# Four graph layers on one core: count one-hots a step further ahead, output projection loads issued earlier, and two convolutions that read their rows from SBUF with the first one's weights split in the stage before

## The chip, the cores and the metric

One core of a Trainium2 chip. The metric is the device time of one execution in microseconds; lower is better. All stretches are given from the start of the profiled span.

## The reference

1250 nodes (padded to 10 tiles of 128), width 768, 20000 edges sorted by target, 34 edge types. Four layers, each followed by a residual and a layer norm:

```python
x = _layernorm(x + _L0(x))   # relu(x W_ah + b), three GAT convolutions of 4 heads, relu(concat @ W_out + b_out)
x = _layernorm(x + _L1(x))   # GCN: h = x @ W; out[col] += dinv[row] * dinv[col] * h[row]; + b
x = _layernorm(x + _L2(x))   # GAT of 12 heads of 64 with a residual projection
x = _layernorm(x + _L3(x))
# _L3:
mean = agg.reshape(N_REL, n, -1) / jnp.maximum(cnt, 1.0).reshape(N_REL, n, 1)
h1 = jnp.einsum('rni,rio->no', mean, W_rel) + x @ W_root + b_rgcn
xw = h1 @ W_gcn
out = jax.ops.segment_sum(xw[src] * norm[:, None], dst, num_segments=n)
out = out + xw * (dinv * dinv)[:, None] + b_gcn
```

## The kernel before

Five engine programs are written out by hand and synchronised by counting semaphores. Between most stages stands `meet` (L165): each engine drains, adds one, and waits for all five. The order of the work is each engine's own program order. The stages, with their rough places in the span:

- **Phase 1** (to 614): `x W_ah`, then the three GAT projections W_H[0..2]. Beside the third, and after it, an N x N table of edge counts is made from 49 groups of 4 x 128 edges. For a group, VectorE makes the source one-hots and type one-hots (`dve_compare`, L796 and L800), ScalarE the target one-hots (`act_targets`, L808, L810), TensorE sums them (`pe_group`, L840, 12 matmuls), ScalarE copies the sum (`act_sums`, L819) and VectorE adds it into the table `ct` (`dve_add`, L827). Per projected tile VectorE also makes the attention reductions (`projected`, L496, L497). Beside each of the last eight tiles there are two groups, one before and one behind the tile's products (L351); 33 groups follow in a loop. VectorE compares one group ahead: group k + 1, then the add of group k.
- **Phase 3 and att0** (to 1242): the table is turned, then 12 heads of attention; POOL stores each head's output into `gat_d` (L1100).
- **Output projection** (`sp_wout`, `act_wout`, `dve_wout`, `pool_wout`; 1242 to 1554): three blocks, l = 0 to 2, each rows `gat_d[l]` times a 768 x 768 block of W_out, added up in `z4` in SBUF. The products are made in split precision: rows and weights are each split in a high and a low part (CAST and subtract, L1433, L1434 by chunks of 128 rows; rows by ScalarE L386 and VectorE L403), and a tile's products are 3 x 6 x 2 = 36 matmuls (L270), behind 6 transposes (L253). SyncE streams row tiles (L221), the next block's weights (L215), and, in the third block, a tile of x (L1414), which waits until an earlier tile is normalised. VectorE empties PSUM (L1458), and in the third block also adds x, norms, and makes a mask (`dve_mask2`, L883) that only the 12-head attention uses. `dve_wout` splits the weights of block 0 first, all six chunks.
- **conv1** (`Convolution`, to 1758): rows x1 are read back from DRAM and transposed; one DMA loads the weights (L209) and VectorE splits them whole (L394, L395); g = dinv * product (L1524, L1567); then the aggregation with count columns (L1554).
- **Heads, att2, root, rel** (to 3716): the 12-head layer and the relation products, which aren't touched, save that the masks come to stand at the front of the heads.
- **Sum** (to 3992): messages are summed into `hbuf` (L1968, L1993). Then `sp_h1` stores h1 to DRAM (L2011), between two meetings.
- **conv3**: the same class as conv1, with rows read back from `h1_d`.

The quoted lines are those that set the order in counting and in the third block:

```python
for k in range(2 * (j - FIRST_TILE), 2 * (j - FIRST_TILE) + 2):
    dve_compare(v, k + 1, (k + 1) % 2)
    dve_add(v, step, k, k % 2)
    if k % 2 == 0:
        projected(2, j, j % 2)
```

## Time and profile before

| what | value |
|---|---|
| median of 3 runs | 4196.65 us (4187.52 to 4201.66) |
| the profiled execution: device time | 4204.77 us |
| its span, first to last instruction | 4203.2 us |
| its mean granted TensorE clock | 0.958 |
| busy in the span | TensorE 3832.1, VectorE 1959.1, ScalarE 1702.1, POOL 1569.5 us |

The profiled execution took 8.1 us more than the median. Busy time is a sum over the span; TensorE's matmuls are pipelined, so that a busy TensorE isn't one at its peak. In a row of a timeline stand the start, the duration, the engine, the line and operation, what is written and read, how many instructions are merged, and in brackets the idle time before it and what ended that.

### The profile page before, as it was taken

To read this page: it belongs to the slowest core of one execution; us is meant where nothing else is said; L and a number is where in the kernel's file an instruction comes from. 1 tells how busy PE (TensorE), PEld (TensorE's weight loads), DVE (VectorE), ACT (ScalarE), POOL (GpSimd) and SP (SyncE) were. 2 spreads that over 40 slices of the span, in tenths; PEclk is the share of its full clock that TensorE was granted. 3 is DMA by queue.
4 is the path that set the end of the run, shared out by engine and by line. 5 is a ranking of instruction groups with operands and counts; after the bars stand their busy time and mean duration, and the time that the engine had idled before them with its cause. 6 is when DMAs were issued, how large, how long until landed. Compare 5 with 4: busy or idle time off the path is not lost. (4 is left out here: it accounts for less than half of the span.)

```text
span 4203.2 us, 58400 instructions
## 1 busy us (share of the span) xinstructions
PE 3832.1 (91%) x18472; PEld 2962.6 (70%) x18473; DVE 1959.1 (47%) x2764; ACT 1702.1 (40%) x2902; POOL 1569.5 (37%) x1191
## 2 busy tenths in 40 slices
PE   8998768999988869869998999999999999989989
PEld 4554336777768859732222699999999999965579
DVE  7245687666633343489996233333333332013325
ACT  1113576766653212149988133333333333310021
POOL 3887873444430000101111244444444444357600
PEclk9998998999998979979999999999999999999989
DMA  4332111222213231231111355555555554368821
GB/s 139 103 106 65 36 23 54 66 66 65 70 53 121 68 108 48 91 106 56 50 50 25 120 184 186 185 184 185 184 180 182 183 181 135 112 221 303 258 86 67
DMA packets 209319, 494.64 MB, mean 118 GB/s; under 512 B 71824, under 2 KB 88231, under 8 KB 209206
## 3 DMA queue, kind: packets, MB, share of 16 engines
q1 hardware_dynamic: 121078, 217.41, 16.0%
q0 software_dynamic: 53568, 181.40, 13.9%
q10 hardware_dynamic: 34560, 94.45, 6.4%
q8 instruction: 56, 0.92, 0.1%
q14 instruction: 57, 0.47, 0.0%
HBM read 365.32 MB, written 127.48 MB: 117 GB/s over the span
## 5 line engine op out<-in xcount | busy, mean ns | idle before, releaser
L1875 PE MATMUL ps<-wsplit,xsplit 128*128 x6840 | 1237.0, 337 | 1.3 <-POOL xsplit L1842 1.3
L1875 PEld LDWEIGHTS ps<-wsplit,xsplit 128*128 128x128 f32 x6840 | 1181.5, 188 | 1.5 <-issue 1.5
L1304 ACT ACTIVATE work<-ps,work 128x418 f32<-128x418 f32 x720 | 435.1, 606 | 241.2 <-PE ps L1214 240.4
L1251 PE MATMUL ps<-hbuf,work 128*128 128x193 f32 x2400 | 494.5, 345 | 13.2 <-DVE work L1166 13.1
L1842 POOL TENSOR_TENSOR xsplit<-ct,xsplit 128x768 fp32r<-128x768 f32 x190 | 370.1, 1948 | 297.6 <-ACTq L1907 297.5
L1149 DVE SCALAR_TENSOR_TENSOR work<-work,cnt 128x1250 f32<-128x1250 f32 x240 | 370.7, 1545 | 229.4 <-ACT work L1304 226.1
L1812 DVE CAST wsplit<-wplain 128x768 fp32r<-128x768 f32 x204 | 115.6, 567 | 761.3 <-PE ps L1875 730.4
L1912 ACT ACTIVATE ct<-ps,invs 128x768 f32<-128x768 f32 x190 | 171.4, 902 | 711.7 <-PE ps L1875 711.7
L1251 PEld LDWEIGHTS ps<-hbuf,work 128*128 128x128 f32 x2400 | 385.3, 191 | 83.3 <-issue 83.3
L1295 ACT ACTIVATE ps<-work,lr 128x418 f32<-128x418 f32 x720 | 418.3, 606 | 5.8 <-DMA work<-lrow_d 5.8
L1837 POOL DMA_INDIRECT ct<-x_d,relrec x190 | 199.1, 1048 | 517.7 <-PE ps L1863 497.3
L1241 PE MATMUL ps<-work,hbuf 128*65 128x512 f32 x720 | 340.4, 556 | 16.7 <-DVE work L1149 16.5
L270 PE MATMUL ps<-wsplit,xsplit 128*128 128x384 f32 x1800 | 343.9, 351 | 12.1 <-DVE xsplit L403 12.1
L270 PEld LDWEIGHTS ps<-wsplit,xsplit 128*128 128x128 f32 x1800 | 330.9, 199 | 14.1 <-DVE xsplit L403 14.1
L1214 PEld LDWEIGHTS ps<-work 3*128 3x128 bf16 x720 | 65.3, 91 | 357.5 <-ACT ps L1295 186.0
L1214 PE MATMUL ps<-work 3*128 3x418 bf16 x720 | 251.8, 351 | 29.3 <-DMA work<-shift_d 26.2
L1348 POOL DMA_INDIRECT invs<-inv_d,relrec x190 | 249.7, 1314 | 65.5 <-issue 57.6
L1968 PE MATMUL ps<-work 128*128 128x384 f32 x784 | 256.1, 490 | 18.8 <-DMA work<-msg_d,work 17.6
L1813 DVE TENSOR_TENSOR wsplit<-wplain,wsplit 128x768 fp32r<-128x768 f32 x204 | 245.9, 1205 | 7.1
L763 POOL DMA_INDIRECT relrec_d<-work x160 | 228.1, 1426 | 48.8 <-issue 48.8
L763 POOL DMA_INDIRECT dstrec_d<-work x160 | 207.0, 1293 | 97.9 <-DVEq L685 49.4
L1968 PEld LDWEIGHTS ps<-work 128*128 128x128 f32 x784 | 149.7, 191 | 124.9 <-issue 23.0
(215 smaller groups left out, 4375.5 us busy)
## 6 DMA issues: line engine op xcount, KB each, us to landing
wplain<-in_L_gnn_W_rel SPq DMA_DIRECT2D x34, 2304.0 KB, 9.7
msg_d<-ct ACTq DMA_DIRECT2D x190, 384.0 KB, 2.6
work<-lrow_d SPq DMA_DIRECT2D x47, 625.0 KB, 3.6
feat_d<-work ACTq DMA_DIRECT2D x30, 386.0 KB, 3.1
hbuf<-feat_d SPq DMA_DIRECT2D x60, 193.0 KB, 2.5
gat_d<-work POOLq DMA_DIRECT2D x12, 960.0 KB, 5.2
xplain<-gat_d SPq DMA_DIRECT2D x30, 384.0 KB, 3.1
work<-xa_d SPq DMA_DIRECT2D x27, 384.0 KB, 3.4
```

Source lines behind the costliest of these rows:

```text
L270: last = pe.matmul(o, x[:, u, c * P:(c + 1) * P], w[:, c * D + h * HALF:c * D + (h + 1) * HALF], start=(q == 0 and c == 0), stop=(q == 2 a ...
L763: g.indirect_dma_start(out=(relrec_d, dstrec_d)[which], out_offset=bass.IndirectOffsetOnAxis(addr[:, which, t:t + 1], 0), in_=(relpay[:, t ...
L1149: v.scalar_tensor_tensor(p[:, 0:N], p[:, 0:N], 1.0, cnt3[:, q % NT, 0:N], ALU.min, ALU.mult).then_inc(self.s_p, 1)
L1214: pe.matmul(ps[:, b, 0:c1 - c0], self.ones3, self.crow[h % 2][:, c0:c1], start=False, stop=True, skip_group_check=True).then_inc(self.s_ad ...
L1241: last = pe.matmul(ps[0:C + 1, 3 + k, 0:n1 - n0], self.feat(h, s), p[:, n0:n1], start=(s == 0), stop=(s == NT - 1))
L1251: last = pe.matmul(ps[:, self.b0 + b, t * (C + 1):(t + 1) * (C + 1)], p[:, dt * P:(dt + 1) * P], self.feat(h, s), start=(s == 0 and t == 0 ...
L1295: act.activation(ps[:, b, 0:c1 - c0], self.Rb[h % 2][:, c0:c1], ACT.Relu, bias=lr[:, col:col + 1]).then_inc(self.s_relu, 1)
L1304: act.activation(self.p[q % 3][:, c0:c1], ps[:, b, 0:c1 - c0], ACT.Exp, bias=self.l2[:, col:col + 1], scale=1.0 - SLOPE)\
L1348: g.indirect_dma_start(out=invs[:, k:k + 1], out_offset=None, in_=inv_d, in_offset=bass.IndirectOffsetOnAxis(relrec[:, 2 * k + 1:2 * k + 2 ...
L1842: g.tensor_tensor(xlo7[:, k % XW, :], xt7[:, k % 2].rearrange("p c n -> p (c n)"), xhi7[:, k % XW, :].bitcast(F32), ALU.subtract).then_inc ...
L1875: last = pe.matmul(ps[:, 4 + 2 * (u % 2) + h, 0:HALF], x[:, u, c * P:(c + 1) * P], w[:, bass.ds(base + (c * D + h * HALF), HALF)], start=( ...
L1968: last = pe.matmul(ps[:, 2 * (u % 2) + h, 0:HALF], sel8[:, GT * (u % 2) + w, :], mg8[:, GT * u + w, h * HALF:(h + 1) * HALF], start=(w == ...
```

## The change

- `dve_compare` is one group further ahead (k + 2 before the add of k).
- Meetings between attention and output projection, between that and conv1, and around the store of h1 are taken out; single waits stand in their place. TensorE opens block 0 before the attention (`open`), and its first transposes come right behind the last attention product.
- SyncE issues the bias columns and row tiles 0 and 1 of block 0 during the last head; the broadcasts of the output bias wait for the last product and the last head's store.
- In block 0 VectorE splits chunk 0, makes the low rows of tile 0, then splits the other five.
- The x tiles of the third block are issued by POOL, behind the x1 store of the tile two before. Into the room of the second projection's weights SyncE loads conv1's weights in pieces (four at tile 0, two at tile 6); VectorE splits one chunk a tile in tiles 3 to 8.
- The ten masks go to the front of the heads stage.
- Both convolutions take their rows from SBUF (`multiply_resident`): conv1 from `z4`, conv3 from `hbuf`. The store and reload of h1 are gone. conv3 splits by chunk.
- Split products run by chunk: six matmuls (two halves, three part products) for a chunk, with a wait for that chunk's split.

```diff
@@ dve_phase1
-            dve_compare(v, 0, 0)
+            for k in range(2):
+                dve_compare(v, k, k)
             for j in range(FIRST_TILE, NT):
                 for k in range(2 * (j - FIRST_TILE), 2 * (j - FIRST_TILE) + 2):
-                    dve_compare(v, k + 1, (k + 1) % 2)
+                    dve_compare(v, k + 2, k % 2)
                     dve_add(v, step, k, k % 2)
@@ class Dense
+            def products(self, pe, j, u):
...
+                    whi, wlo, xhi, xlo, (s_w, s_x), n = self.split
+                    pe.wait_ge(s_x, NT * n + j + 1)
+                    for c in range(KC):
+                        pe.wait_ge(s_w, KC * n + c + 1)
+                        for h in range(2):
+                            for q, (x, w) in enumerate(((xhi, whi), (xhi, wlo), (xlo, whi))):
+                                last = pe.matmul(ps[:, 4 + 2 * u + h, 0:HALF], x[:, u, c * P:(c + 1) * P],
...
@@ sp_wout
+            sp.wait_ge(att0.s_max, NT * att0.H)
+            for u in range(2):
+                sp.wait_ge(att0.s_stored[u], 16 * 2)
             for l in range(3):
                 for j in range(NT):
                     W_OUT[l].stream_tile(sp, j, j % 2, P)
                     if l == 0 and j == 1:
+                        sp.wait_ge(att0.s_agg, NT * att0.H)
+                        for u in range(2):
+                            sp.wait_ge(att0.s_stored[u], 16 * (att0.H // 2))
...
-                    if l == 2:
-                        if j < 2:
-                            sp.wait_ge(W_OUT[1].product, W_OUT[1].all_products)
+                    if l == 2 and j in (0, 6):
+
+                        if j == 0:
+                            sp.wait_ge(s_split4, 3 * KC)
                         else:
-                            sp.wait_ge(s_z4, j - 1)
-                        n = tile_rows(j)
-                        sp.dma_start(x4s[0:n, j % 2, :], a["x"][j * P:j * P + n, :]).then_inc(s_x4s[j % 2], 16)
-            conv1.dense.load(sp)
+                            sp.wait_ge(conv1.s_w, 2)
+                        for c in range(4) if j == 0 else (4, 5):
+                            sp.dma_start(wplain[:, (c % 4) * D:(c % 4 + 1) * D], a["L1_gnn_W"][c * P:(c + 1) * P, :]).then_inc(conv1.dense.w_in, 16)
@@ dve_wout
                     if j + 2 < NT:
                         d.low_rows(v, (j + 2) // 2, j % 2)
+                    elif l == 2 and j == NT - 1:
+                        v.sem_inc(conv1.dense.emptied, 2)
+                        conv1.dense.low_rows(v, 0, 0)
+                    if l == 2 and 3 <= j < 3 + KC:
+                        c = j - 3
...
+                        conv1.dense.split_chunk(v, step, c, wplain[:, (c % 4) * D:(c % 4 + 1) * D])
@@ pool_wout
                 g.dma_start(x1_d[j * P:(j + 1) * P, :], z4[:, j, :]).then_inc(s_z4st[j % 2], 16)
+                if j + 2 < NT:
+                    n = tile_rows(j + 2)
+                    g.dma_start(x4s[0:n, j % 2, :], a["x"][(j + 2) * P:(j + 2) * P + n, :]).then_inc(s_x4s[j % 2], 16)
@@ Convolution.pe, act, dve
-                self.dense.multiply(pe)
+                self.dense.multiply_resident(pe, self.rows, lambda j: self.ready(pe, j))
...
+                    if self.n == 0:
+                        act.wait_ge(s_z4st[u], 16 * (i + 1))
...
-                d.split_weights(v, step)
...
+                if self.n == 1:
+                    v.sem_inc(d.emptied, 2)
+                    v.wait_ge(d.w_in, d.b[d.pick] + 16)
+                    d.split_chunk(v, step, 0, d.w_at[:, 0, :])
+                    d.low_rows(v, 0, 0)
+                    for c in range(1, KC):
+                        d.split_chunk(v, step, c, d.w_at[:, c, :])
+                d.low_rows(v, 0, 1)
```

How the instructions stand now. VectorE, in counting, around the reductions of the first tile with groups beside it; L796, L800 are a group's one-hots, L496, L497 the reductions, L827 the add. Before:

```order
L496 TENSOR_TENSOR work<-work 128x768 [waits dve_step]
L497 TENSOR_REDUCE lr<-work 128x4 [waits dve_step]
L796 TENSOR_TENSOR hbuf<-iota,drec 128x4x34 [waits dve_step,count_products]
L800 TENSOR_SCALAR hbuf<-iota,drec 128x1280 x4
L824 TENSOR_LOAD group_dst
L824 ISA x2
L827 ISA [waits counts_summed]
L827 TENSOR_TENSOR ct<-hbuf,ct 128x1314
```

Now (L799, L803 and the like are the same lines, three or four further down), with the group of the next tile in front of the reductions:

```order
L800 TENSOR_TENSOR hbuf<-iota,drec 128x4x34 [waits count_products]
L804 TENSOR_SCALAR hbuf<-iota,drec 128x1280 x4
L828 TENSOR_LOAD group_dst [waits tables_cleared]
L828 ISA x2
L831 ISA [waits counts_summed]
L831 TENSOR_TENSOR ct<-hbuf,ct 128x1314
L499 TENSOR_TENSOR work<-work 128x768 [waits dve_step,h_tile_ready]
L500 TENSOR_REDUCE lr<-work 128x4 [waits dve_step]
```

The comparison that followed the reductions, and for which TensorE waited, now stands before the add and the reductions.

SyncE in the third block of the output projection (L221 and now L220 are row tiles). Before, one x load after each row tile:

```order
L1414 DMA work<-in_x 128x768 [waits dense_product]
L221 DMA xplain<-gat_d 128x768 [waits dense_turned]
L1414 DMA work<-in_x 128x768 [waits x1_ready]
L221 DMA xplain<-gat_d 128x768 [waits dense_turned]
L1414 DMA work<-in_x 128x768 [waits x1_ready]
```

Now:

```order
L1426 DMA wplain<-in_L_gnn_W 128x768 [waits wout_weights_split]
L1426 DMA wplain<-in_L_gnn_W 128x768 x3
L220 DMA xplain<-gat_d 128x768 [waits dense_turned] x6
L1426 DMA wplain<-in_L_gnn_W 128x768 [waits conv_w_split]
L1426 DMA wplain<-in_L_gnn_W 128x768
L220 DMA xplain<-gat_d 128x768 [waits dense_turned] x3
```

The waits for a normalised tile (x1_ready) have left this queue; two waits for splits have come.

VectorE from the last add of the sum to the second convolution. Before:

```order
L1993 TENSOR_TENSOR hbuf<-ps,hbuf 128x768
L394 CAST wsplit<-work 128x4608 [waits dve_step,met,dense_w_in1]
L395 TENSOR_TENSOR wsplit<-work,wsplit 128x4608 [waits dve_step]
L403 TENSOR_TENSOR xsplit<-xplain,xsplit 128x768 [waits dve_step,dense_product,dense_taken]
L403 TENSOR_TENSOR xsplit<-xplain,xsplit 128x768 [waits dense_product,dense_taken]
```

Now, of the five further chunks the first:

```order
L2031 TENSOR_TENSOR hbuf<-ps,hbuf 128x768
L397 CAST wsplit<-work 128x768 [waits dve_step,dense_w_in1]
L398 TENSOR_TENSOR wsplit<-work,wsplit 128x768 [waits dve_step]
L406 TENSOR_TENSOR xsplit<-xplain,xsplit 128x768 [waits dve_step,dense_product,dense_taken]
L397 CAST wsplit<-work 128x768
L398 TENSOR_TENSOR wsplit<-work,wsplit 128x768 [waits dve_step]
```

The wait for the meeting (met) is gone, and the low rows come after one chunk's split.

## Rows read from the trace of the kernel before

**Rows 1.** Timeline of TensorE in the counting, 430 to 500 us.

```profile
447.51 2.41 PE L840 MATMUL ps<-hbuf 128*128 128x512 bf16 x12
...
453.72 3.90 PE L840 MATMUL ps<-hbuf 128*128 128x512 bf16 x12 [3.15 <-DVE hbuf L800]
457.46 7.90 PE L351 MATMUL ps<-work 128*128 128x384 f32 x24
```

**Rows 2.** Waits of TensorE, 340 to 496: us in total, times, longest.

```profile
PE ps L840 <- DVE hbuf L800: 32.0, 9, 5.5
```

**Rows 3.** Timelines of ScalarE and VectorE at the same place.

```profile
449.96 1.26 ACT L819 ACTIVATE hbuf<-ps 128x1314 uint16<-128x1314 f32 x1 [1.37 <-PE ps L840]
...
452.81 0.30 DVE L796 TENSOR_TENSOR hbuf<-iota,drec 128x136 bf16<-128x136 uint16 x1
```

**Rows 4.** Groups by line, 494 to 614: busy us, mean ns, idle before.

```profile
L840 PE MATMUL ps<-hbuf 128*128 128x512 bf16 (+1 forms) x387 | 79.5, 351 | 40.0 <-DVE hbuf L800 40.0
L800 DVE TENSOR_SCALAR hbuf<-iota,drec 128x1280 bf16<-128x1280 uint16 x128 | 72.9, 630 | 0.0
```

**Rows 5.** Timeline of TensorE, 1225 to 1345.

```profile
1234.40 7.46 PE L1251 MATMUL ps<-hbuf,work 128*128 128x193 f32 x44
...
1280.38 1.54 PE L253 MATMUL ps<-ident,xplain 128*128 128x128 f32 x6 [6.72 <-DMA xplain<-gat_d]
```

**Rows 6.** POOL and SyncE there; the drain (ns); landing (page, DMA issues).

```profile
1245.12 1.01 POOL L1100 DMA_DIRECT2D gat_d<-work  x1 [23.96 <-DVEq L1169]
...
1257.14 9.01 SPq L1403 DMA_DIRECT2D hbuf<-in_L_gnn_b_out  x10
...
L167 POOLq DRAIN  x1: 4075/4075/4075, 1250.4 to 1250.4; - x1
...
gat_d<-work POOLq DMA_DIRECT2D x12, 960.0 KB, 5.2
```

**Rows 7.** The third block as one window: busy times, clock, DMA share, GB/s.

```profile
1423.20:1554.10 130.90, 87.86 (x421) 84.51 (x420) 51.37 (x93) 28.11 (x80) 4.36 (x8) 0.79 0.29 90
```

**Rows 8.** Waits of SyncE's queue, 1423 to 1554.

```profile
SPq L1414 <- DVEq L1466: 114.2, 8, 20.0
```

**Rows 9.** Timeline of TensorE: steady tiles of block two, first of block three.

```profile
1368.89 6.51 PE L270 MATMUL ps<-wsplit,xsplit 128*128 128x384 f32 x36
...
1375.81 6.52 PE L270 MATMUL ps<-wsplit,xsplit 128*128 128x384 f32 x36
...
1431.52 8.77 PE L270 MATMUL ps<-wsplit,xsplit 128*128 128x384 f32 x36 [0.67 <-DVE xsplit L403]
```

**Rows 10.** Timeline of VectorE: a third-block tile, and two chunks' splits.

```profile
1254.49 0.56 DVE L1433 CAST wsplit<-wplain 128x768 fp32r<-128x768 f32 x1 [9.73 <-POOLq L167]
...
1256.08 0.56 DVE L1433 CAST wsplit<-wplain 128x768 fp32r<-128x768 f32 x1
...
1443.60 0.96 DVE L403 TENSOR_TENSOR xsplit<-xplain,xsplit 128x768 fp32r<-128x768 f32 x1 [2.32 <-ACT xsplit L386]
...
1448.73 0.95 DVE L1458 TENSOR_TENSOR hbuf<-ps,hbuf 128x768 f32<-128x768 f32 x1
```

**Rows 11.** DMA issues, 1440 to 1563: KB each, median us to landing.

```profile
x_d<-hbuf POOLq DMA_DIRECT2D x10, 384.0 KB, 5.4
```

**Rows 12.** Timeline of TensorE: the first convolution's first products.

```profile
1572.12 8.09 PE L270 MATMUL ps<-wsplit,xsplit 128*128 128x384 f32 x36 [2.80 <-DVE xsplit L403]
```

**Rows 13.** The chain that ended last: start, us, what.

```profile
3992.78 10.84 DMA h_d<-hbuf
...
4012.66 8.08 PE ps L270 x36
```

**Rows 14.** The masks (ns); POOL and VectorE at the heads.

```profile
L883 DVE TENSOR_SCALAR ct<-ct x10: 489/494/497, 1434.4 to 1553.6; 128x1280 bf16<-128x1280 uint16 x10
...
1762.26 6.60 POOL L1633 MEMSET hbuf<- 128x7800 f32 x1 [0.15 <-POOL work L1631]
...
1777.02 0.96 DVE L496 TENSOR_TENSOR work<-hbuf,work 128x768 f32<-128x768 f32 x1 [13.19 <-ACTq L1703]
```

More of the change, by code:

```diff
@@ L313, in turn @@
                     last.then_inc(self.turned, 1)
-                def times(j):
-                    pe.wait_ge(self.taken, self.b["taken"] + j + 1)
-                    pe.wait_ge(self.emptied, self.b["emptied"] + j + 1)
-                    for h in range(2):
-                        for c in range(KC):
-                            last = pe.matmul(ps[:, 4 + 2 * (j % 2) + h, 0:HALF], self.xt_at[:, j % 2, c, :],
-                                             self.weight(c)[:, h * HALF:(h + 1) * HALF], start=(c == 0), stop=(c == KC - 1))
-                    last.then_inc(self.product, 1)
                 turn(0)
@@ L327, in multiply_resident @@
                         turn(j + 1)
-                    times(j)
+                    self.products(pe, j, j % 2)
             def multiply_single(self, pe, between):
@@ L404, in low_rows, with take_and_empty @@
                  .then_inc(s_x, 1)
-            def take_and_empty(self, act, loop, per, empty, before=None):
-                for u in range(2):
+            def take_and_empty(self, act, loop, per, empty, before=None, taken=0):
+                for u in range(taken, 2):
                     self.take(act, 0, u)
@@ L1444, in dve_wout @@
                 v.sem_inc(d.emptied, 2)
-                for j in range(2):
-                    d.low_rows(v, j // 2, j % 2)
+                if l == 0:
+                    split(0, 0)
+                    d.low_rows(v, 0, 0)
+                    for c in range(1, KC):
+                        split(0, c)
+                    d.low_rows(v, 0, 1)
+                    v.wait_ge(s_root, 1)
+                    step(v.reciprocal(dinv[:, :], dinv[:, :]))
+                else:
+                    for j in range(2):
+                        d.low_rows(v, 0, j)
                 for j in range(NT):
                     z = z4[:, j, :]
-                    if l == 2:
-                        dve_mask2(v, step, j)
                     if l == 1 and j == 6:
                         v.wait_ge(W_OUT[0].product, W_OUT[0].all_products)
+                    if l == 0 and j == 6:
+                        for u in range(2):
+                            v.wait_ge(att0.s_stored[u], 16 * (att0.H // 2))
                     for c in {6: (0, 1), 7: (2, 3), 8: (4,), 9: (5,)}.get(j, ()) if l < 2 else ():
@@ L1468, in pool_wout @@
         def pool_wout(g, step):
+            g.wait_ge(s_split4, 3 * KC)
+            for j in range(2):
+                g.dma_start(x4s[:, j, :], a["x"][j * P:(j + 1) * P, :]).then_inc(s_x4s[j], 16)
             for j in range(NT):
@@ L1510, in sp @@
             def sp(self, sp):
[L1511 removed]
+                sp.wait_ge(self.s_emptied, self.at2 + 1)
                 sp.dma_start(self.brow, self.bias.partition_broadcast(P)).then_inc(self.s_b_in, 16)
@@ L2033, in _ @@
                 W_OUT[0].load_piece(sp, c)
-            meet(sp)
             sp_wout(sp)
-            meet(sp)
+            for u in range(2):
+                sp.wait_ge(s_z4st[u], 16 * (NT // 2))
             conv1.sp(sp)
@@ L2112, in _ @@
             self_loops(v, step, ALU.subtract)
+            for j in range(NT):
+                dve_mask2(v, step, j)
             dve_heads(v, step)
```

168 lines of the change are left out of this document (71 added, 97 removed).

## The prediction

> **What bounds the kernel now.** I read the chain of waits first, then the idle time of TensorE by releaser, then the timelines of the places that the diff touches. TensorE is the engine that the other four feed; what the change can win is idle or slow TensorE time, and there are five places.
>
> *Counting.* Each tile of the third GAT projection has two count groups beside it. The group behind the tile's products runs at once (2.41 us). The next one starts 6.21 us after it (447.51 to 453.72), waits 3.15 us for VectorE and then takes 3.90 us, since its one-hots come only then [rows 1]. Over the stretch TensorE waited nine times for them, 32.0 us [rows 2]. The one-hots stand behind the projection's reductions in VectorE's order: they begin at 452.81, while the ScalarE copy that the group needs too is out at 449.96 + 1.26 = 451.22 [rows 3]. In the 33 groups after the projection VectorE alone paces: TensorE waits 40.0 us for 128 comparisons of 630 ns [rows 4].
>
> *Attention to output projection.* The last attention product ends at 1234.40 + 7.46 = 1241.86. The second row tile's products come only after 1280.38, because the third tile's transposes, which stand before them, wait for their rows until then [rows 5]. Those rows are queued behind ten broadcasts of the bias, issued from 1257.14, after a meeting that waited for a 4.08 us drain of POOL; the last head's store was issued at 1245.12 and landed 5.2 us later [rows 6].
>
> *Third block of the output projection.* From 1423.20 to 1554.10 TensorE is busy 87.86 of 130.90 us at a granted clock of 0.79 [rows 7]. The chain is SyncE's: it waits 114.2 us for a normalised tile before it issues the x load, and the next row load stands behind that [rows 8]. Elsewhere a tile takes 1375.81 - 1368.89 = 6.92 us, 6.51 of it products [rows 9].
>
> *First convolution.* Its products begin at 1572.12, 18.0 us after the projection's last at 1554.10 [rows 7, 12]: a meeting, a reload of rows, a split of all weights.
>
> *Second convolution.* The same with a store: 10.84 us for h1 to land, first products at 4012.66 for 8.08 us, that is to 4020.7 [rows 13].
>
> **The change part by part.** All sums are against the profiled execution (span 4203.2, device time 4204.8).
>
> 1. *One-hots two groups ahead.* No instruction is added. Eight of the nine late groups (all but the first, which has nothing before it) find theirs ready. Such a group then starts when the copy of the preceding group is out: 451.22 against 453.72, 2.5 us sooner, and runs 2.41 instead of 3.88 to 4.54 (3.90 here), on average 1.8 less; 8 x 4.3 = 34. A tile's period shrinks by about 4 us; VectorE's comparisons for two groups (2 x 4 x 0.63 = 5 us by rows of the tail [rows 4]) and its adds and reductions still fit into what is left, by my estimate. In the tail VectorE stays the bound and wins only the comparison that it no longer has to make there, about 2 us, partly the same time as the last group's gain. I take 35; bounds 28 (the copy or the target one-hots become late) and 38. POOL's scatter of the relation records, which runs beside all this, is not shortened; nothing in the attention waits for it but POOL's own head stores behind its gathers, which the first head hides. Without that cover up to the whole 35 would be lost.
>
> 2. *Row tiles 0 and 1, the bias columns and the weight pieces before the attention ends, no meeting.* The broadcasts now wait for the last head's store itself, 1245.12 + 5.2 = 1250.3 instead of 1257.14: 6.8 us. Ten broadcasts, a weight piece and the third row tile took (1280.38 - 1257.14) / 12 = 1.94 us each; the two row tiles issued just ahead of them no longer compete, up to 3.9 us, of which I take 1.6 since they had a head start: 8.4. Tile 0's products come long before, but tile 1 stays behind the third tile's rows, so the rest of the earlier start buys nothing. What is late next is again these rows. Bounds 6 and 10.
>
> 3. *x loads on POOL's queue.* The row loads are now held by TensorE alone. Added: SyncE issues four conv weight pieces between row tiles 0 and 1, and two between tiles 6 and 7, the last two behind the second split. Start: tile 1's rows now follow four pieces, so products begin some 10.5 us after the block's start instead of 8.3, at 1431.52 [rows 9]. Ten tiles: a cold first of 8.5 and nine of 6.9, 71. The wait for the second split costs once: VectorE makes it about 7.4 us after tile 4's products end, then come two issues, two pieces and the row tile, landing at about 13, where the transposes want it at 6.9; 6 us, and 1.5 of slow clock after it. VectorE: from the low rows at 1443.60 to the next add at 1448.73 is 5.1, 0.5 of it the mask that leaves, and some 1.1 from that add to the next low rows: 5.7 per tile; each of the six splits adds 1.59 (1254.49 to 1256.08) [rows 10]: 7.3 against 6.92, so it falls behind by some 3 us in all, of which I charge 1. Sum 10.5 + 71 + 7.5 + 1 = 90 against 130.9: 41. Bounds 32 and 48. The x loads have some 11 us between issue and use; POOL's stores of the same size landed in a median of 5.4 us [rows 11], so they are hidden. If they took over 11, the tile would follow them.
>
> The row is clear that the wait on the normalised tile, and not the transfers, stretches the tiles: the 16 DMA engines are busy 0.29 of the block [rows 7]. [...]
>
> 4. *First convolution from SBUF, weights split before.* The store's landing, the meeting, the row loads and the split of all weights leave the path. What stays: VectorE's norm of tile 8, the add of tile 9 and the low rows come before the first product. With VectorE some 4 us behind, that is 7.4 us after the last projection product, against 18.0 [rows 12]: 10.6. Bounds 7 and 13.
>
> 5. *Masks.* Ten of 0.49 us move from step 3's block to the front of the heads, beside POOL's 6.60 us fill and before VectorE's first reduction, which idled 13.19 us [rows 14]. VectorE's side is covered. The fill could be slowed, which would hold up ScalarE: 0 to 3.5 us, I take 1.
>
> 6. *Second convolution from SBUF.* The last add ended just before the store's issue at 3992.78 [rows 13]. Now one chunk's split (1.6), the transposes and copies beside it, low rows at about 3996.7; the products of tile 0 then follow the other five splits, 5 x 1.59, and end at about 4005.9 instead of 4020.7: 14.8. Less 1 for a clock that may still be low in the next tile. Bounds 11 and 16.
>
> 7. *Products by chunk instead of by half.* 36 matmuls a tile as before, banks changed every three matmuls, a wait per chunk. [...] So nothing; bounds 0 and 0.2 us a tile, 10 in all.
>
> Sum: 35 + 8.4 + 41 + 10.6 - 1 + 13.8 = 107.8, rounded to 108. The span becomes 4095. The profiled execution stood 8.1 us above the median of the runs shown (4196.65), so I forecast 4196.65 - 108 = 4089.
>
> **The rivals.**
>
> *A: the third block stays held.* Row loads pass, but another wait takes over: x rows late on POOL's queue, or VectorE's chain of low rows, split and norm with its step waits at 9 to 10 us a tile instead of 7.3. For it: VectorE gets 9.5 us of splits and loses 4.9 of masks there. Against: VectorE needs 7.3 us of the 14 that a tile takes now. With 3 us a tile more on seven tiles the gain falls by 21: 4110.
>
> *B: counting wins little.* The first group's one-hots are ready but the pace moves to ScalarE's copy and target one-hots, or to the tail. For it: the tail is VectorE's. Against: ScalarE ended its work for the waiting group 1 us and more before VectorE did [rows 3]. Half the term: 4107.
>
> *C: slower than before.* The chunk order breaks TensorE's pace: each change of bank and each wait leaves a gap, and the granted clock falls to the lower level in stretches that now run at the higher. The products of 50 tiles are touched. It decides from 108 / 50 = 2.2 us a tile, 8.7 us instead of 6.51; at 12 us (wholly at the lower clock, about twice the present) it would be 5.5 x 50 = 275 slower, less 108: 4364. A tile after an idle already takes 8.08 [rows 13], so the range is not absurd. [...]
>
> *D: it doesn't do what it says:* a first wait on something that is as late as the removed meeting (for instance the head's store for the bias, the x1 stores before the new g tiles), so that terms 2, 4 and 6 vanish: 33 less, 4122.
>
> **How the numbers follow.** Forecast 0.68, A 0.12, B 0.09, D 0.06, C 0.03, and 0.02 for A, B and D together or anything near no change. What a measurement of this kernel can tell is about 0.3%, 13 us; all cases but C and the last lie far beyond it. So faster 0.95, same 0.01, slower 0.04. The bounds of the terms give 4196.65 less 84 minus 13.5 for masks and chunk waits, 4126, and less 125, 4072. The range takes in A and B, and D's and the lower bound only in part: 4070 to 4118.
>
> **What would show it.** Right: TensorE's waits for the comparisons down from 32 to about 10 us in the counting; attention starting some 35 us sooner; tile 1 of the output projection near 1273 on the old time axis; a third block of about 90 us with one gap of about 6 us before its seventh or eighth tile; the convolution's first products about 7 us after the block; the second convolution's tile 0 stretched over 9 us beside the splits. Wrong: a product tile over 6.6 us in the steady stretches (C), gaps in front of every tile of the third block (A), a first count group per tile still paced by comparisons (B), or a median above 4118.

## The result, and the profile after

| | before | changed kernel |
|---|---|---|
| median | 4194.36 us (4187.52 to 4201.66, 4 runs) | 4102.81 us (4096.95 to 4104.04, 4 runs) |
| ratio | | 0.9779, 95% interval 0.9766 to 0.9792 |
| profiled execution: device time, span | 4204.8, 4203.2 | 4104.0, 4102.4 |
| its mean granted clock | 0.958 | 0.968 |

The medians differ by 91.6 us and the profiled spans by 100.8. The forecast of 4089 us was 14 us too fast. With the lines of the changed kernel (L840 is now L844, L796 is L800, L800 is L804, L819 is L823, L351 is L354, L270 is L298, L253 is L261, L167 is L166), in the order of the rows of before:

*Counting.* Timeline of TensorE, one tile of the third projection (start, duration, engine and line, idle before it in brackets):

```profile
372.68 2.41 PE L844 MATMUL ps<-hbuf 128*128 128x512 bf16 x12
...
376.67 2.19 PE L844 MATMUL ps<-hbuf 128*128 128x512 bf16 x11 [0.93 <-ACT hbuf L823]
378.70 7.90 PE L354 MATMUL ps<-work 128*128 128x384 f32 x24
386.44 2.41 PE L844 MATMUL ps<-hbuf 128*128 128x512 bf16 x12
```

and its waits from 340 to 464 us (total, times, longest):

```profile
PE ps L844 <- ACT hbuf L823: 6.9, 7, 1.4
PE ps L844 <- DVE hbuf L804: 5.8, 1, 5.8
```

The second group starts 3.99 us behind the first instead of 6.21 and runs at full pace, against [rows 1]. What it waits for now, 0.93 us, is ScalarE's copy of the preceding group's sum (L823), as the forecast had it. The comparisons still hold TensorE up once (5.8 us, the first group), where [rows 2] had nine waits of 32.0 us together. A tile's period fell from 465.20 - 447.51 = 17.7 to 386.44 - 372.68 = 13.8 us, and the last count addition ended at 580.43 + 0.84 = 581.27, where it had ended at 615.18: 33.9 us sooner.

*Attention to output projection.* Timeline of TensorE:

```profile
1208.39 0.82 PE L261 MATMUL ps<-ident,xplain 128*128 128x128 f32 x6
...
1222.82 1.33 PE L298 MATMUL ps<-wsplit,xsplit 128*128 128x384 f32 x6 [0.37 <-DVEq L399]
1238.73 1.54 PE L261 MATMUL ps<-ident,xplain 128*128 128x128 f32 x6 [14.58 <-DMA xplain<-gat_d]
```

Tile 0's products run beside the weights' split, one chunk at a time, and then TensorE idles 14.58 us for row tile 2, which still stands behind the ten bias broadcasts. From the attention's end (1208.56) to these transposes it is 30.2 us, against 38.5 in [rows 5].

*Third block.* The window of the block, and the timeline of TensorE in it:

```profile
1380.40:1469.65 89.25, 74.51 (x421) 73.23 (x420) 52.72 (x88) 27.64 (x79) 8.79 (x16) 0.89 0.42 140
```

```profile
1390.52 1.54 PE L261 MATMUL ps<-ident,xplain 128*128 128x128 f32 x6 [5.54 <-DMA xplain<-gat_d]
1391.71 8.60 PE L298 MATMUL ps<-wsplit,xsplit 128*128 128x384 f32 x36
...
1400.72 6.49 PE L298 MATMUL ps<-wsplit,xsplit 128*128 128x384 f32 x36
...
1407.62 6.51 PE L298 MATMUL ps<-wsplit,xsplit 128*128 128x384 f32 x36
...
1441.03 1.54 PE L261 MATMUL ps<-ident,xplain 128*128 128x128 f32 x6 [6.17 <-DMA xplain<-gat_d]
...
1476.45 8.87 PE L298 MATMUL ps<-wsplit,xsplit 128*128 128x384 f32 x36 [5.04 <-DVE xsplit L406]
```

The block takes 89.25 us instead of the 130.90 of [rows 7], at a granted clock of 0.89 instead of 0.79. A steady tile takes 1407.62 - 1400.72 = 6.9 us. Products begin 11.3 us after the start, and one gap of 6.17 us is left, in front of tile 7. The last row is the first convolution's first product, 6.8 us behind the block where it was 18.0 [rows 12].

*What the forecast had not.* VectorE, TensorE and GpSimd's drains (ns) around the first meeting that is left, and the drain of the last one:

```profile
1672.75 2.11 DVE L1770 TENSOR_TENSOR cnt<-cnt,ident 128x128 uint16<-128x128 uint16 x10 [10.15 <-POOLq L166]
1674.90 8.95 DVE L887 TENSOR_SCALAR ct<-ct 128x1280 bf16<-128x1280 uint16 x10
1687.31 0.96 DVE L499 TENSOR_TENSOR work<-hbuf,work 128x768 f32<-128x768 f32 x1 [3.46 <-ACTq L1740]
```

```profile
1679.49 2.96 PE L1704 MATMUL ps<-ident,work 128*128 128x128 f32 x12 [21.80 <-DMA work<-x_d]
```

```profile
L166 POOLq DRAIN  x2: 40/3280/6520, 1666.2 to 1680.0; - x2
...
L166 POOLq DRAIN  x1: 8392/8392/8392, 4093.5 to 4093.5; - x1
```

In the kernel before, the same places read:

```profile
1761.72 2.11 DVE L1733 TENSOR_TENSOR cnt<-cnt,ident 128x128 uint16<-128x128 uint16 x10 [4.21 <-POOLq L167]
```

```profile
1768.29 2.01 PE L1667 MATMUL ps<-ident,work 128*128 128x128 f32 x8 [15.67 <-DMA work<-x_d]
```

```profile
L167 POOLq DRAIN  x2: 46/452/859, 1760.8 to 1769.0; - x2
...
L167 POOLq DRAIN  x1: 859/859/859, 4201.8 to 4201.8; - x1
```

In both of these meetings all engines wait for GpSimd's drain. Behind the first convolution it lasted 0.86 us and lasts 6.52 now, so that the heads start 21.8 us behind the aggregation instead of 15.7. At the program's end it lasted 0.86 us and lasts 8.39: from the last store's issue to the end of the span it is 4102.4 - 4090.37 = 12.0 us, where it was 4203.2 - 4198.71 = 4.5. (The first of the ten masks, L887, took 5.33 us and ended at 1680.23; GpSimd's fill beside it ran from 1673.29 to 1679.89, and the other nine masks took 0.48 us each. The fill kept its 6.60 us. So in this run it was the mask that was longer beside the fill, not the fill beside the masks, as term 5 allowed.)

*Second convolution.* Timeline of TensorE:

```profile
3899.26 1.53 PE L324 MATMUL ps<-ident,hbuf 128*128 128x128 f32 x12 [1.22 <-DVEq L2032]
3903.02 2.66 PE L298 MATMUL ps<-wsplit,xsplit 128*128 128x384 f32 x12 [2.23 <-DVE xsplit L406]
...
3911.14 1.31 PE L298 MATMUL ps<-wsplit,xsplit 128*128 128x384 f32 x6 [0.37 <-DVEq L399]
```

Tile 0 ends at 3912.45, 14.4 us behind the sum's last matmul (3898.05), where it was 4020.74 - 3991.51 = 29.2.

### The profile page after: what moved, and what is told of

Its sections match the earlier page's. It is cut to its first block, busy times and chain, and to the rows that moved or that the text cites. A ratio compares the mean times of both kernels' runs of the same rounds, so it can differ in the third digit from the quotient of the medians.

```text
span 4102.4 us, 58268 instructions
## 1 busy us (share of the span) xinstructions
PE 3794.5 (92%) x18463; PEld 2939.7 (72%) x18473; DVE 1965.1 (48%) x2784; ACT 1702.3 (41%) x2902; POOL 1577.8 (38%) x1201
## 4 chain that ended last, share of the span: by engine, by line
PE 43%; POOL 5%; DVE 5%; issue 3%; ACT 1%; DMA 0%; SPq 0%; DVEq 0%; ACTq 0%; POOLq 0%
PE ps L1913 29%; POOL work L1995 5%; PE ps L1245 3%; PE ps L1901 3%; PE ps L1587 3%; DVE work L1125 2%; PE ps L306 2%; PE ps L298 1%; DVE work L1153 1%; PE ps L1218 1%; ACT work L1308 1%; PE ps L324 0%; DMA work<-msg_d,work 0%; ACT ps L1299 0%; DVE mask L1762 0%
## 5 line engine op out<-in xcount | busy, mean ns | idle before, releaser
L1255 PE MATMUL ps<-hbuf,work 128*128 128x193 f32 x2400 | 494.5, 345 | 13.2 <-DVE work L1170 13.1
L298 PE MATMUL ps<-wsplit,xsplit 128*128 128x384 f32 x1800 | 336.3, 344 | 13.9 <-DVE xsplit L406 11.8
L298 PEld LDWEIGHTS ps<-wsplit,xsplit 128*128 128x128 f32 x1800 | 320.9, 194 | 17.2 <-issue 7.7
L1352 POOL DMA_INDIRECT invs<-inv_d,relrec x190 | 240.8, 1267 | 60.0 <-issue 57.6
L767 POOL DMA_INDIRECT relrec_d<-work x160 | 241.9, 1512 | 48.8 <-issue 48.8
```

Of the source, the lines that this page charges most:

```text
L298: last = pe.matmul(ps[:, 4 + 2 * u + h, 0:HALF], x[:, u, c * P:(c + 1) * P], w[:, c * D + h * HALF:c * D + (h + 1) * HALF], start=(q == 0 ...
L767: g.indirect_dma_start(out=(relrec_d, dstrec_d)[which], out_offset=bass.IndirectOffsetOnAxis(addr[:, which, t:t + 1], 0), in_=(relpay[:, t ...
L1255: last = pe.matmul(ps[:, self.b0 + b, t * (C + 1):(t + 1) * (C + 1)], p[:, dt * P:(dt + 1) * P], self.feat(h, s), start=(s == 0 and t == 0 ...
```

## The experiments

The kernels ran on three chips in three groups, each timed beside the kernel before, whose median was 4219.4, 4193.4 and 4222.1 us in them. The difference lies in one stage that no kernel here alters: from first to last matmul the sum of the messages takes 257 to 259 us on the second and 281 to 285 on the other two. So I compare ratios, or stages within profiles. By the changed kernel's ratio of 0.9771 to 0.9779 its time on the first chip would be 4123 to 4126 us.

**Counting alone** (e1_count_alone: the kernel before with the changed order of comparisons).

```
-                    dve_compare(v, k + 1, (k + 1) % 2)
+                    dve_compare(v, k + 2, k % 2)
                     dve_add(v, step, k, k % 2)
```

> The kernel before with the counting order alone (comparisons of a group issued two groups ahead of the addition that uses them, instead of one). If the profile's account of the changed kernel is right, the counting's period falls from 17.7 us a pair to 13.8, the last addition ends 34 to 36 us earlier (615.2 to about 580), nothing behind it gives any of this back, and the time is 4194.4 - 35 = 4159 us (4157 to 4162). Rival (B of the prediction): the gain is partly bought elsewhere in the changed kernel, and the counting alone gives 17 us or less: 4177 or more.

Measured: 4188.7 us beside 4219.4, ratio 0.9929 (0.9915 to 0.9942), 31 us less, by the interval 24 to 36. The count groups run from 347.6 to 580.3 where they ran from 344.8 to 612.6 (their first and last start): 35.1 us shorter. Waits of TensorE from 340 to 496:

```profile
PE ps L841 <- DVE hbuf L801: 13.1, 7, 5.5
PE ps L841 <- ACT hbuf L820: 5.6, 7, 1.4
```

So the counting has its gain alone, and rival B falls. My expectation counted from 4194.4, the median of another chip; against its own before the run gives 31 where I expected 35, inside the interval.

**x loads back in SyncE's queue** (e3b_x_on_sp).

```
 W_OUT[l].stream_tile(sp, j, j % 2, P)
...
+if l == 2:
+    if j < 2:
+        sp.wait_ge(s_split4, 3 * KC)
+    else:
+        sp.wait_ge(s_z4, j - 1)
+    n = tile_rows(j)
+    sp.dma_start(x4s[0:n, j % 2, :], a["x"][j * P:j * P + n, :]).then_inc(s_x4s[j % 2], 16)
...
-    g.dma_start(x4s[0:n, j % 2, :], a["x"][(j + 2) * P:(j + 2) * P + n, :]).then_inc(s_x4s[j % 2], 16)
```

> The changed kernel with the loads of x for the third block back in SyncE's queue, between the row tiles, each behind its wait for the row tile of two before to be ready (GpSimd issues the stores alone, with a wait for its own store of two tiles before, which has long landed). Theory: this wait in SyncE's in-order queue was what held the third block at 13.1 us a tile, since the next row tile's load stands behind it; 8 steps go from 6.9 back to some 12 to 13 us, the block goes from 89 to 125 to 131 us, and the time to 4102.8 + 38 = 4141 us (4136 to 4145). Rival: the block was held by the masks and by the four-stage chain of a row tile itself, and the move of the loads is worth little: under 4115.

Measured: 4175.4 us, ratio 0.9893 (0.9877 to 0.9908), some 50 us above the changed kernel. The waits of SyncE's queue from 1383 to 1520 and TensorE's timeline there:

```profile
SPq L1425 <- DVEq L1495: 124.1, 8, 22.8
```

```profile
1444.35 1.54 PE L261 MATMUL ps<-ident,xplain 128*128 128x128 f32 x6 [3.80 <-DMA xplain<-gat_d]
...
1459.70 1.54 PE L261 MATMUL ps<-ident,xplain 128*128 128x128 f32 x6 [5.57 <-DMA xplain<-gat_d]
```

The old picture [rows 8] is back, the wait of 114.2 us is 124.1, and a tile takes 1459.70 - 1444.35 = 15.4 us: more than the 13.1 of before, since VectorE now makes the convolution's splits in the same chain (the tile before this one, the last without a split, takes 1444.35 - 1430.82 = 13.5). The rival (masks and the row tile's own chain) falls; the price of the wait was higher than I expected.

**Masks back in the third block** (e4_masks_back).

```
+if l == 2:
+    dve_mask2(v, step, j)
...
-for j in range(NT):
-    dve_mask2(v, step, j)
 dve_heads(v, step)
```

> The changed kernel with the ten mask operations of 0.6 to 0.9 us back in the third block on VectorE. Theory: the later start of the heads (21.8 us behind the aggregation against 15.7) is the drain of GpSimd and not the masks, which lie beside the fill of GpSimd (6.60 us) that VectorE waits for anyway: the heads' start stays at 21.8 us +- 0.5. In the third block VectorE has room (6.9 us a tile set by other work), so the block grows by 0 to 3 us: time 4102.8 + 0 to 4 = 4103 to 4107. Rival: the masks cost the 6 us in front of the heads, and without them there the time is 4097 us.

Measured: 4124.65 us, ratio 0.9775 (0.9762 to 0.9789), no difference from the changed kernel. The heads still start late:

```profile
1676.62 3.18 PE L1706 MATMUL ps<-ident,work 128*128 128x128 f32 x12 [21.54 <-DMA work<-x_d]
```

From the projection's first to last transposes it is 246.8 us, 248.1 to 248.5 in two profiles of the changed kernel. The ten masks took 0.49 us each in the block, less than the 0.6 to 0.9 of my expectation. So the masks cost nothing that these runs can tell in either place, and are not what made the heads late.

**Drains ahead of time** (e2_drain_early).

```
 def pool(self, g, step):
+    g.drain()
     store_tiles(g, step, self.s_ready, self.z, self.out_dram, self.stored, self.at)
```

> The changed kernel with one more drain on GpSimd at the start of each of the two convolutions, while it waits for the first row tile to store. Theory (the drain's debt): a drain of GpSimd lasts as long as the DMAs it has issued since the last one make it, some 86 ns each (10 stores 0.86 us in three meetings of the kernel before), wherever it stands; the change removed meetings whose drains lay beside other work, so that the drains of the meetings behind the two convolutions became 6.52 and 8.39 us long and both lie on the path to the end. With the early drains those two fall back to about 0.86 us, the heads' first transposes start 15.7 to 16.2 us behind the aggregation's end instead of 21.8, and the time falls by 5.7 + 7.5 = 13 us: 4102.8 - 13 = 4090 us (4088 to 4092). Rival: the long drains wait for something else (the last stores' landing, the masks that stand in front of the heads now), and stay as long as they are: 4102.8 +- 1.

Measured: 4109.7 us, ratio 0.9738 (0.9725 to 0.9752), against the changed kernel 13 to 16 us less. The drains (ns) of the added line, then of the meetings, then TensorE's start of the heads:

```profile
L1650 POOLq DRAIN  x1: 5703/5703/5703, 1481.3 to 1481.3; - x1
...
L1650 POOLq DRAIN  x1: 16687/16687/16687, 3893.1 to 3893.1; - x1
...
L166 POOLq DRAIN  x2: 46/456/867, 1663.0 to 1671.2; - x2
...
L166 POOLq DRAIN  x1: 869/869/869, 4106.9 to 4106.9; - x1
```

```profile
1670.68 2.82 PE L1705 MATMUL ps<-ident,work 128*128 128x128 f32 x12 [16.22 <-DMA work<-x_d]
```

The 6.52 us have split into 5.70, paid at 1481 where GpSimd waits for the first row tile, and 0.87 behind the convolution's ten stores. The heads start 16.2 us behind the aggregation, and the end has its 0.87 us back. One more piece of evidence comes from e3b, where GpSimd issues ten loads less before the same meeting: 5.71 us there instead of 6.52, or 81 ns for each. The 86 ns a DMA of my expectation were an estimate, 0.86 us over ten stores, and as a price for all of them they don't hold: in front of the 5.70 us GpSimd had issued 546 DMAs, which would make 47 us. What these runs show is what ten more or less make (0.81 us), and that the time moves with the drain.

**The store of the sum, and its meetings, back** (e5_h1_back). The store only costs; the rows still come from SBUF.

```
+def sp_h1(sp):
+    sp.dma_start(h1_d.rearrange("(j p) n -> p j n", p=P), ...).then_inc(s_h1, 16)
+    sp.wait_ge(s_h1, 16)
...
+meet(sp)
+sp_h1(sp)
+meet(sp)
 conv3.sp(sp)
```

> The changed kernel with the store of the sum to DRAM and the two meetings around it back in front of the last convolution, which still takes its rows from SBUF and splits its weights as the changed kernel does. The store serves nobody; it is there for its price. Theory: the store (10.84 us in the chain of the kernel before) and the two meetings add 12 to 13.5 us between the sum's last matmul and the first product (5.0 us in the changed kernel, 17 to 18.5 here), and the drain in the second meeting pays GpSimd's debt of the gathers beside the sum, so that the last drain is 0.86 us instead of 8.39: +13 - 7.5 = +5.5 us against the changed kernel (+4 to +7). Rival (no debt; the last drain is long because the kernel ends there): +13 us.

Beside it ran the changed kernel itself:

> The changed kernel once more, unaltered, as the reference for the runs beside it on this chip. Its ratio to the kernel before should be 0.978 (0.9766 to 0.9792), its drains behind the two convolutions 6.5 and 8.4 us, and, if the chip is the one of the four runs before these, the stage that sums the messages some 24 us longer than in the first profiles (282 us from first to last matmul against 258), in this kernel and in the kernel before alike.

Measured: a_again 4097.2 us beside 4193.4, ratio 0.9771 (0.9758 to 0.9785), drains of 6.52 and 8.39 us; the sum takes 257.1 us there, so it was not the chip of the first group. e5_h1_back 4105.1, ratio 0.9793 (0.9780 to 0.9806), 7.9 us above it by the medians, a little over the 4 to 7 expected, and 4.9 by the two profiled spans. In the profiles, from the sum's last matmul start to the last product start of the convolution's dense part it is 3891.5 to 3979.4, 87.9 us, against 3890.0 to 3966.1, 76.1: +11.8. The last drain is short again (ns):

```profile
L167 POOLq DRAIN  x1: 867/867/867, 4098.2 to 4098.2; - x1
```

and from the aggregation's last matmul start to the span's end it is 4099.6 - 4089.1 = 10.5 us against 4094.7 - 4076.8 = 17.9: -7.4. Both halves of the theory hold: what comes back in front of the convolution costs 11.8 us, and 7.4 of it are returned at the end.

**Products by half again** (e6_by_half).

```
-for c in range(KC):
-    pe.wait_ge(s_w, KC * n + c + 1)
-    for h in range(2):
-        for q, (x, w) in enumerate(((xhi, whi), (xhi, wlo), (xlo, whi))):
+pe.wait_ge(s_w, KC * n + KC)
+for h in range(2):
+    for q, (x, w) in enumerate(((xhi, whi), (xhi, wlo), (xlo, whi))):
+        for c in range(KC):
```

> The changed kernel with the 36 products of a tile in the old order (by half of the output, then by part, then by chunk; one wait for all six weight chunks). Theory (term 7 at zero): a tile's products last 6.5 us in either order, the granted clock is the same, and only the first tiles of the first block and of the last convolution lose what the wait for six chunks instead of one costs them (1 to 7 us each, since six splits of 1.7 us stand in front): +4 to +12 us in all. Rival C turned round (the order by chunk costs TensorE pace at each change of bank): the tiles become shorter than 6.5 us, and the time falls.

Measured: 4107.5 us, ratio 0.9798 (0.9785 to 0.9812), 10.3 us above a_again. Timeline of TensorE, steady tiles of the third block and the start of the second convolution:

```profile
1396.29 6.49 PE L298 MATMUL ps<-wsplit,xsplit 128*128 128x384 f32 x36
...
1403.19 6.51 PE L298 MATMUL ps<-wsplit,xsplit 128*128 128x384 f32 x36
...
3905.60 8.19 PE L298 MATMUL ps<-wsplit,xsplit 128*128 128x384 f32 x36 [10.44 <-DVEq L399]
```

A tile takes 6.49 to 6.51 us in either order, to the hundredth. What the order by chunk buys is the start of a block: the convolution waits 10.44 us for all six splits, and from the sum's last matmul start to the last product start it is 83.1 us against 76.1. In the first block the same wait (10.52 us) is free, since row tile 2 is later still: its transposes start 30.4 us behind tile 0's here, 30.3 in the changed kernel.

**A better version** (e8_three_waits), with the early drains and three edits of SyncE's order.

```
-for t in range(NT):
-    sp.dma_start(z4[:, t, :], a["L0_gnn_b_out"].partition_broadcast(P)).then_inc(s_b4, 16)
+sp.dma_start(z4[:, NT - 1, :], a["L0_gnn_b_out"].partition_broadcast(P)).then_inc(s_b4, 16)
...
-if l == 2 and j in (0, 6):
+if l == 2 and j in (1, 8):
...
-step(v.tensor_tensor(halves(z), d.psum(j % 2), halves(z), ALU.add))
+step(v.tensor_tensor(halves(z), d.psum(j % 2), halves(z if l else z4[:, NT - 1, :]), ALU.add))
```

The wait for the attention's last stores also moves, from the broadcasts to the second block.

> A better version of the changed kernel, made from what the two profiles show: the early drains of e2, and three edits of SyncE's order in the output projection. (1) One broadcast of the output bias (into the last tile's place) instead of ten, added from there by every tile of the first block; the wait for the last stores of the attention moves to the second block. Row tile 2's transposes waited 14.6 us: they should start at 1224 to 1226 instead of 1238.7, gain 11 to 14.5 us. (2) The first four pieces of the convolution's weights one row tile later: the wait of 5.5 us for row tile 1 of the third block goes or shrinks to 1 us, gain 4 to 5.5 us. (3) The wait for the second split and the last two pieces at row tile 8 instead of 6: the gap of 6.2 us goes, gain 5 to 6.2 us. With 13 us (up to 17 by the ratio) for the drains, against the changed kernel: -33 to -43 us, a ratio to the kernel before of 0.968 to 0.970. Rival: the transfers moved collide with others and two of the three gaps come back elsewhere: -20 us or less.

Measured: 4067.0 us, ratio 0.9695 (0.9682 to 0.9708), 30 us below a_again on the same chip. Timeline of TensorE at the first row tiles, in the third block and behind it:

```profile
1224.96 0.88 PE L261 MATMUL ps<-ident,xplain 128*128 128x128 f32 x6 [3.04 <-DMA xplain<-gat_d]
...
1370.11 1.54 PE L261 MATMUL ps<-ident,xplain 128*128 128x128 f32 x6 [3.64 <-DMA xplain<-gat_d]
1372.21 1.54 PE L261 MATMUL ps<-ident,xplain 128*128 128x128 f32 x6 [0.56 <-DMA xplain<-gat_d]
1375.33 8.63 PE L298 MATMUL ps<-wsplit,xsplit 128*128 128x384 f32 x36 [1.57 <-DVE xsplit L406]
...
1440.50 6.48 PE L298 MATMUL ps<-wsplit,xsplit 128*128 128x384 f32 x36 [1.26 <-DVE xsplit L406]
...
1454.85 8.15 PE L298 MATMUL ps<-wsplit,xsplit 128*128 128x384 f32 x36 [6.11 <-DVE xsplit L406]
```

Row tile 2 now waits 3.04 us, and both gaps of the third block are gone. From the first to the last transposes of the projection it takes 226.5 us (1206.2 to 1432.7) against 248.1, 21.6 less. But TensorE now runs ahead of VectorE, which gives 3.0 us back between there and the aggregation (1528.3 - 1432.7 = 95.6 against 92.6). The drains give 4.8 and 7.5. The sum of these, 30.9, agrees with the medians (30) and misses the lower end of what I expected (33) by 2 to 3: the edits won what they should at their places, but the next engine took some of it.

**Doses** (e9_drain_doses: e8 with drains at chosen distances).

```
 low(k)
+if k in (3, 7, 15, 31, 63, 159):
+    g.drain()
```

> The better version (e8) with six more drains of GpSimd inside the stage that gathers rows for the relation's messages, behind row tile 3, 7, 15, 31, 63 and 159 of 190, that is 4, 8, 16, 32 and 96 gathers apart (the gather of a tile is issued four tiles ahead). Theory (a debt by the number of DMAs, some 82 to 86 ns each as with stores): these drains last about 0.35, 0.7, 1.35, 2.7 and 8 us, and the one in the meeting behind the stage, 26 gathers after the last, 2.2 us instead of 8.35. The meeting's drain ended beside TensorE's last products in every profile so far, so its being shorter gives nothing; the drains inside stand in GpSimd's queue before the row tiles' low parts, with 4 rows of lead: 0 to 8 us lost, time 4067 to 4075. Rival (a cap: a drain costs at most about 8.35 us however many DMAs, since 200 and 206 DMAs gave 8.35 and 8.39 us where 82 ns each would be 16 to 17): then the long ones stop growing at 8.35, which 96 gathers cannot tell from the theory but the six together can: if the short ones are in proportion and the first, with the DMAs of three stages before it, is the 8.35, the debt is per DMA with a cap near 100 of them.

Measured: 4089.6 us beside 4222.1, ratio 0.9689 (0.9675 to 0.9702), the same as e8. The drains (ns) behind tiles 7, 15, 31, 63 and 159, and that of the meeting:

```profile
L1891 POOLq DRAIN  x1: 2417/2417/2417, 2314.9 to 2314.9; - x1
...
L1891 POOLq DRAIN  x1: 2604/2604/2604, 2370.2 to 2370.2; - x1
...
L1891 POOLq DRAIN  x1: 3259/3259/3259, 2480.9 to 2480.9; - x1
...
L1891 POOLq DRAIN  x1: 5016/5016/5016, 2702.2 to 2702.2; - x1
...
L1891 POOLq DRAIN  x1: 9792/9792/9792, 3366.2 to 3366.2; - x1
...
L166 POOLq DRAIN  x1: 3926/3926/3926, 3573.5 to 3573.5; - x1
```

The drain behind tile 3, after ten stores and eight gathers, took 3.83 us. These drains are longer than expected by some 2 us each. The timeline of GpSimd shows what those are, here at the drains behind tile 7 and tile 159 and at the meeting's:

```profile
2314.96 1.93 POOL L1881 TENSOR_TENSOR xsplit<-ct,xsplit 128x768 fp32r<-128x768 f32 x1 [1.12 <-ACTq L1948]
...
3366.28 1.84 POOL L1881 TENSOR_TENSOR xsplit<-ct,xsplit 128x768 fp32r<-128x768 f32 x1 [1.65 <-ACTq L1948]
...
3573.40 1.84 POOL L1881 TENSOR_TENSOR xsplit<-ct,xsplit 128x768 fp32r<-128x768 f32 x1 [4.79 <-ACTq L1948]
```

GpSimd's own low part of the row tile, issued just before the drain, runs for the first 1.8 to 2.3 us of each of them. What is left behind it is 0.45, 0.72, 1.38, 2.68 and 7.91 us after 4, 8, 16, 32 and 96 gathers, and 2.19 us in the meeting after 26: 82 to 90 ns a gather from 8 on, where ten stores took 0.86 us. So from 8 gathers on these drains agree with the estimate of 82 to 86 ns, the meeting's among them; after 4 gathers it is 112 ns each, and behind tile 3 some 1.9 us are left for 18 DMAs, 108 ns each. A gather is in flight at the drains inside the stage and lands 1.9 to 4.1 us after their start, so that for the short ones the landing could be the bound as well; in the meeting none is (the last was issued 30 us before), and the price is the same. One thing stays open. 190 gathers and 10 stores without a drain between give 8.35 us in every kernel here, of which again 1.7 to 1.9 are the low part: about 6.6 us, less than the 7.91 after 96, where 200 x 83 ns would be 16.6. Up to where the drain grows, and on what that hangs, these runs don't tell. That the meeting's drain was 4.4 us shorter gave nothing: from the messages' last product to the sum's first it is 16.3 us (3589.3 to 3605.6), 16.0 in the changed kernel, since TensorE comes to that meeting after the drain.

## Why the prediction was right, and where not

| term | predicted | measured in the two profiles |
|---|---|---|
| 1 counting | 35 | 33.9 |
| 2 attention to projection | 8.4 | 8.3 |
| 3 third block | 41 | 41.6 |
| 4 first convolution's start | 10.6 | 11.2 |
| 5 heads' start | -1 | -6.1 |
| 6 second convolution's start | 13.8 | 14.8 |
| 7 order by chunk | 0 | 0 |
| the program's end | not in the sum | -7.5 |
| all other stretches together | 0 | +4.4 |
| sum | 108 | 100.6 of 100.8 |

**Terms 1 to 4 and 6** came out within 1.1 us each, by the mechanisms named. In the order of term 2, the broadcasts of the bias start 8.5 us behind the attention instead of 15.3, and from there to row tile 2 it is 21.7 us instead of 23.2: the 6.8 and 1.6 of the forecast. The one gap of the third block is 6.17 us (6 forecast, in front of its seventh or eighth tile), products begin 11.3 us after its start (10.5), the convolution's first product 6.8 behind it (7.4). The x loads landed in a median of 4.1 us, far below the 11 at which the tile would have followed them. In term 6 the forecast took 1 us off for a slow clock in the next tile; it runs in 6.51 us, so the charge was needless.

**The step that failed** is the cost of a removed meeting. In part 2 I read the 4.08 us drain of GpSimd as work that the meeting made, gone with it. In these runs the time behaved as a debt that the next drain collects: in e2 it was paid as 5.70 us at 1481, and the meeting's own drain fell from 6.52 to 0.87. The drains removed lay at 1250 (4.08 us), at 1562 (0.87) and beside the sum (22.55 us, ended before the sum did). The first two stood on the path, and terms 2 and 4 have the gain of their going; but it is only lent, for the meeting behind the first convolution now collects it, 5.7 us more than before, about 4.08 + 0.87 of it for these two and 0.8 for the ten x loads that GpSimd now issues. The third lay beside other work and cost nothing; what it cleared is collected by the last meeting, where all engines stand and wait, 7.5 us. The forecast put nothing for either and gave no reason for that. e2 shows it by moving the debt, e5 by putting one collector back. The measured -6.1 in the row of term 5 has nothing to do with the masks of term 5 (e4), which are worth 0.

**Term 7** was put at 0, with a bound of 0.2 us a tile, by an estimate; no run on record then shows either. What the runs show in its place is e6: 6.49 to 6.51 us a tile in both orders.

**The standing of the profiled run** made the other half of the miss: of the 14.2 us between 4088.6 and 4102.8, 7.2 are the sum of the terms (107.8 against 100.6) and 6.9 the step from spans to medians. I took the full sum from the median of before. But the profiled execution before stood 10.4 us above the median of the four runs, and that of after only 1.2 above its own, so that a sum of stages that explains 100.8 us between two profiles is 91.6 between two medians. Most of the 4.4 us of the other stretches are a part of that: from the heads' first matmul to the sum's first it is 1964.2 us in the profile of before, 1960.6 in that of after, and 1960.3 in e1, which has the code of before there. I had named the 8.1 us and not put them in the range as an error of their own; the range held the time because it reached for A and B. That is luck in part: nothing in it was meant for the drains, and their 12.6 us (5.1 beyond what term 5 had put aside, and 7.5) were made smaller by 5.4 us that the other rows gave above the forecast.

**The rivals.** A: no tile of the steady part waits; e3b shows that the removed wait was the cause, at 50 us. B: falls by e1. D: each first wait came as soon as assumed, to 1 us. C: tiles take 6.49 to 6.51 us in either order (e6), the granted clock of the whole span is 0.968 with both, and from 1248.1 to 1289.0 in the profile of after, where the banks change every three matmuls, TensorE is busy all 40.90 us at a granted clock of 1.00. The lower clock that this rival reckons with is in the trace of before, 0.50 from 1427 to 1436 against 1.00 from 1438 to 1449; the steady tiles of the changed kernel's third block, 1400.7 to 1407.2 and 1407.6 to 1414.1, ran at 1.00.

## What to carry to other kernels

When a change removes a meeting or moves DMAs onto GpSimd, ask where GpSimd drains next and how many DMAs it will have issued by then; a drain placed where it idled cost nothing here (e2). In a queue look for the wait, not for the transfer: SyncE's stood 114.2 us of the third block's 130.90 in front of x loads, with the DMA engines busy 0.29 of it [rows 7, 8], and 124.1 us in e3b, where each row load again came behind such a wait. And a sum of stages read from one profile is a difference between profiles; before it is taken from a median, say how the profiled run stands to it, and widen the range by that.

## What the runs showed of the hardware that was not expected

Up to 96 DMAs, GpSimd's drains were longer the more of them it had issued since its last one; over more they were not (7.91 us after 96, 4.08 after 526). As measured:

| run | DMAs since the drain before | drain, us |
|---|---|---|
| before, at 1769.0 | 0 | 0.05 |
| before, three meetings | 10 stores | 0.87, 0.86, 0.86 |
| e9 | 10 stores and 8 gathers | 1.9 beyond GpSimd's own work |
| e9 | 4, 8, 16, 32, 96 gathers | 0.45, 0.72, 1.38, 2.68, 7.91 beyond it |
| e9, the meeting | 26 gathers | 2.19 beyond it |
| after, the meeting at 3608.3 | 190 gathers, 10 stores | 8.35, about 6.6 beyond it |
| after, the end | 196 gathers, 10 stores | 8.39 |
| before, at 1250.4 | 526 | 4.08 |
| e2; e3b | 546 | 5.70; 5.71 |
| after, at 1666.2 | 556 | 6.52 |

From 8 gathers to 96 that is 82 to 90 ns each, and from 546 to 556 DMAs 81; over the whole count of the last five rows it is 8 to 42 ns each. The DMAs need not be in flight for it: in front of e9's meeting the last gather was issued 30 us before the drain, and these gathers landed 3.9 to 7.1 us after their issue. What sets the length these runs don't tell. In the meetings of before VectorE's drains took 10 to 17 ns, GpSimd's up to 22.6 us, the longest with gathers still in flight (it started at 3967.2, the last gather was issued at 3972.88).

The stage that sums the messages took 257 to 259 us on one chip and 281 to 285 on two others, for the same instructions. In it the DMA engines moved 291 GB/s in the one (a_again) and 266 in the other (e4), and TensorE was idle for 1.5 us of it in the one and 20.2 in the other. Why is open.
